# Layer 1 of a four-layer network: router and low-rank columns moved behind the FFN's in one three-bank product, expert choice one pair later

## The reference, cut to what matters

```
base_out   = h @ base_w.T + base_b          # 1024 columns
res_hidden = h @ A.T                        # R1 = 64 columns (low rank)
logits     = h @ router_w.T                 # E1 = 16 columns (router)
topw, topi = top_k(softmax(logits), 2);  topw = topw / (sum(topw) + 1e-6)
combine    = sum over the two chosen experts of one_hot(topi) * topw
out        = base_out + 0.5 * einsum(combine, res_hidden, B)      # B: 16 x 1024 x 64
```

## Time and profile before

| | us |
|---|---|
| median of three runs (lowest, highest) | 2204.11 (2204.09, 2206.6) |
| the profiled execution, whole | 2207.09 |
| its span, first to last instruction | 2205.3 |
| TensorE busy in the span | 2032.4 (92%) |
| VectorE / ScalarE / GpSimd busy | 1183.8 / 885.6 / 388.3 |
| mean granted TensorE clock | 0.964 |

### The profile page before, as it was taken

The page is one execution under the profiler, slowest core; times in us unless marked ns, Lnnn a source line. Parts: engine busy times, 40 slices in busy tenths (PEclk is TensorE's granted clock), DMA queues, the critical chain, the costliest instruction groups (busy, mean ns, idle before and its releaser), DMA issues. The chain is left out here.

```text
span 2205.3 us, 29894 instructions
## 1 busy us (share of the span) xinstructions
PE 2032.4 (92%) x9742; PEld 1665.3 (76%) x9750; DVE 1183.8 (54%) x1986; ACT 885.6 (40%) x1366; POOL 388.3 (18%) x463
## 2 busy tenths in 40 slices
PE   4899956899999979997999999988999999979998
PEld 4777723788888868886788888867888778858886
DVE  6888888745445443224644445436555444454443
ACT  4577722444433321002433333324666544413441
POOL 4122211111111100012111111111000033342334
PEclk9999989899999989997999999998999999989999
DMA  7666546321112232224311111212111011132114
GB/s 185 187 182 181 167 162 216 101 75 57 57 57 71 63 124 76 77 95 135 99 57 57 57 57 61 63 49 81 29 38 33 15 53 50 46 132 78 50 43 156
DMA packets 96302, 196.97 MB, mean 89 GB/s; under 512 B 16768, under 2 KB 46976, under 8 KB 95488
## 3 DMA queue, kind: packets, MB, share of 16 engines
q1 hardware_dynamic: 94976, 194.40, 28.2%
q10 hardware_dynamic: 1280, 1.97, 0.4%
HBM read 142.27 MB, written 54.07 MB: 89 GB/s over the span
## 5 line engine op out<-in xcount | busy, mean ns | idle before, releaser
L936 PE MATMUL ps<-l_u_hi,l_g_hi 128*128 128x512 f32 x512 | 208.9, 408 | 15.7 <-DVE l_u_lo L1270 10.1
L1100 ACT ACTIVATE l_hs<-ps,l_EY,dem3e 128x512 f32<-128x512 f32 x128 | 99.2, 778 | 302.4 <-PE ps L936 292.4
L936 PE MATMUL ps<-l_u_lo,l_g_hi 128*128 128x512 f32 x512 | 204.7, 400 | 0.0
L936 PE MATMUL ps<-l_u_hi,l_g_lo 128*128 128x512 f32 x512 | 204.2, 399 | 0.0
L119 POOL TENSOR_TENSOR l_hs<-l_EY,ones 128x4 f32<-128x4 f32 x128 | 35.0, 273 | 860.1 <-ACT l_hs L1100 860.1
L989 PE MATMUL ps<-l_w_hi,l_h_hi 128*128 128x512 f32 x512 | 167.7, 409 | 0.0
L989 PE MATMUL ps<-l_w_lo,l_h_hi 128*128 128x512 f32 x512 | 163.7, 401 | 0.0
L989 PE MATMUL ps<-l_w_hi,l_h_lo 128*128 128x512 f32 x512 | 163.1, 400 | 0.0
L2228 POOL TENSOR_TENSOR f_a_lo<-f_prod,f_a_hi 128x512 fp32r<-128x512 f32 (+1 forms) x88 | 113.8, 1293 | 269.2 <-ACT f_a_hi L2131 269.2
L2184 DVE SCALAR_TENSOR_TENSOR f_prod<-ps,b,f_gate 128x512 f32<-128x512 f32 (+1 forms) x88 | 66.0, 750 | 170.0 <-ACT f_gate L2124 170.0
L1270 DVE SCALAR_TENSOR_TENSOR l_u_lo<-ps,s_u,l_u_hi 128x512 fp32r<-128x512 f32 x128 | 95.5, 749 | 89.1 <-ACT l_u_hi L1082 88.9
(11 more groups left out here) (326 smaller groups left out, 4892.3 us busy)
## 6 DMA issues: line engine op xcount, KB each, us to landing
xin<-x SPq DMA_DIRECT2D x96, 256.0 KB, 4.0
l_xr<-x SPq DMA_DIRECT2D x32, 512.0 KB, 4.6
x<-l_xr SPq DMA_DIRECT2D x32, 512.0 KB, 2.6
v<-in_ffn_v SPq DMA_DIRECT2D x84, 128.0 KB, 2.7
xin<-in_x SPq DMA_DIRECT2D x16, 512.0 KB, 5.5
xb<-in_x SPq DMA_DIRECT2D x16, 512.0 KB, 3.2
x<-xb SPq DMA_DIRECT2D x16, 512.0 KB, 2.6
q_xr<-x SPq DMA_DIRECT2D x16, 512.0 KB, 3.9
```

The costliest lines, as they stand in the source:

```text
L936: mm = nc.tensor.matmul(ps[:, 3 + h, :], Gs[ws][:, h, at:at + P], Us[ms][:, h, 1 + q:1 + q + HALF], start=(k == 0), stop=(k == 11))
L1100: nc.scalar.activation(hs[:, h, :], ps[:, 3 + h, :], ACT.Identity, bias=EY[:, 1, 0, bass.ds(h * NP + p, 1)], scale=dem3e[:, bass.ds(h * NP ...
```

## The change

1. The weights of layer 1 become one matrix of 1104 columns: FFN 0 to 1023, then the low-rank and the router columns. `ffn` multiplies it in three products of THIRD = 368 columns, into banks 5, 6 and 7. The small product is gone.
2. The expert choice is taken out of the tail into the functions `route` (VectorE) and `route_exp` (ScalarE), with one step less at its start. Pair p−1's choice is made in the tail of pair p, pair 15's in `expert_delta`.
3. The end of the tail: a copy of the 80 small columns out of bank 7, the sum of banks 5 and 6 (736 columns), a wait for that one, the sum of bank 7's other REST = 288 columns.
4. Tiles that the choice needs now live through both phases; some semaphores are counted from another start.

```diff
+THIRD = (L + R1 + E1) // 3
+REST = L - 2 * THIRD
+ROUTE_LINKS = 13
...
-            wsp = sb2("w", [P, KB, L])
-            both_m = sb("m", [P, KB, 2 * SMALL[layer]], F32R)
+            if layer == 1:
+                wsp = sb2("w", [P, KB, 3 * THIRD])
+                msp = [t[:, :, L:3 * THIRD] for t in wsp]
...
                 if first and layer < 3:
                     wait_lo(pe, 0)
+                if layer == 1:
+                    if not first:
+                        pe.wait_ge(xo_ready, r0 + p)
+                    for b in range(KB):
+                        if first:
+                            wait_lo(pe, b + 1)
+                        for ws, ms in PASSES:
+                            for o in range(3):
+                                mm = nc.tensor.matmul(ps[:, 5 + o, 0:THIRD], hsp[ws][:, b, :],
+                                                      wsp[ms][:, b, o * THIRD:(o + 1) * THIRD],
+                                                      start=(k == 0), stop=(k == 3 * KB - 1))
+                            k += 1
+                    mm.then_inc(ffn_done, 1)
+                    return
...
             def tail(p):                      # ScalarE
-                if layer == 1:
-                    act.wait_ge(side[0], side0[0] + p + 1)
-                    nc.scalar.activation(ex[:, :], small[:, R1:R1 + E1], ACT.Exp, bias=nmax[:, :],
-                                         accum_out=esum[:, :]).then_inc(side[1], 1)
+                if layer == 1 and not (isinstance(p, int) and p == 0):
+                    route_exp(nc, act, kept, p - 1, sem)
...
                 if layer == 1:                # VectorE, tail(p)
-                    dve.wait_ge(small_done, r0 + p + 1)
-                    link(0, v.tensor_copy(small[:, :], ps[:, 7, 0:SMALL[1]]))
-                    link(1, v.tensor_tensor(small[:, :], small[:, :],
-                                            ps[:, 7, SMALL[1]:2 * SMALL[1]], ALU.add))
...
+                    if not (isinstance(p, int) and p == 0):
+                        route(nc, dve, kept, p - 1, sem)
+                    dve.wait_ge(ffn_done, r0 + p + 1)
+                    v.tensor_copy(kept["small"][:, :], ps[:, 7, REST:THIRD]).then_inc(small_read, 1)
+                    dve.wait_ge(xr_biased, r0 + p + 1)
+                    planes = in_planes(xr[:, :])
+                    x2 = planes[:, :, 0:THIRD].rearrange("p s (c m) -> p s c m", c=2)
+                    by_rest = planes[:, :, THIRD:HALF]
+                    v.tensor_tensor(x2, ps[:, 5:7, 0:THIRD].rearrange("p c (m s) -> p s c m", s=2), x2,
+                                    ALU.add).then_inc(x_part, 1)
+                    dve.wait_ge(x_part, r0 + p + 1)
+                    dve.wait_ge(small_read, r0 + p + 1)
+                    v.tensor_tensor(by_rest, ps[:, 7, 0:REST].rearrange("p (m s) -> p s m", s=2), by_rest,
+                                    ALU.add).then_inc(xo_ready, 1)
+                    return
...
+def route(nc, dve, kept, p, sem):
...
+    dve.wait_ge(sem("small_read"), p + 1)
+    carry(0)
+    link(0, v.max(top[:, :], small[:, R1:R1 + E1]))
+    v.tensor_copy(kept["res"][:, bass.ds(p, 1), :], small[:, 0:R1].unsqueeze(1))
+    v.tensor_scalar(nmax[:, :], top[:, 0:1], -1.0, None, ALU.mult).then_inc(nmax_ready, 1)
+    dve.wait_ge(ex_ready, p + 1)
+    link(1, v.reciprocal(den[:, 0:1], esum[:, :]))
...
+    link(12, v.tensor_tensor(kept["comb"][:, bass.ds(p, 1), :].rearrange("p a e -> p (a e)"),
+                             prob[:, :], ex[:, :], ALU.add))
...
+def route_exp(nc, act, kept, p, sem):
+
+    act.wait_ge(sem("side0"), p + 1)
+    nc.scalar.activation(kept["ex"][:, :], kept["small"][:, R1:R1 + E1], ACT.Exp, bias=kept["nmax"][:, :],
+                         accum_out=kept["esum"][:, :]).then_inc(sem("side1"), 1)
...
                 split_b(k)                    # expert_delta, ScalarE
+            route_exp(nc, act, kept, NP - 1, sem)
             hi(1, 1, True)
...
                                 ALU.subtract).then_inc(b_lo, 1)      # expert_delta, VectorE
+            route(nc, dve, kept, NP - 1, sem)
             lo(1, 1)
             build(2, 0, False)
```

More of the change, by code:

```diff
@@ L210, in program @@
                     keep_sb("b_raw", [P, AHEAD, L], F32)
+                    keep_sb("small", [P, SMALL[1]], F32)
+                    for name, width in (("iota", E1), ("top", 8), ("nmax", 1), ("ex", E1), ("esum", 1), ("prob", E1),
+                                        ("indexf", 2), ("den", 2), ("pick", 2), ("carrier", 3)):
+                        keep_sb(name, [P, width], F32)
+                    keep_sb("index", [P, 8], U32)
                 if layer == 3:
@@ L566, in conv_phase @@
         if with_ffn:
-            carrier = sb("carrier", [P, 3])
             bias = sb("bias", [P, L])
-            wsp = sb2("w", [P, KB, L])
-            both_m = sb("m", [P, KB, 2 * SMALL[layer]], F32R)
-            msp = [both_m[:, :, i * SMALL[layer]:(i + 1) * SMALL[layer]] for i in range(2)]
-            small = sb("small", [P, SMALL[layer]])
+            if layer == 1:
+                wsp = sb2("w", [P, KB, 3 * THIRD])
+                msp = [t[:, :, L:3 * THIRD] for t in wsp]
+            else:
+                carrier = sb("carrier", [P, 3])
+                wsp = sb2("w", [P, KB, L])
+                both_m = sb("m", [P, KB, 2 * SMALL[2]], F32R)
+                msp = [both_m[:, :, i * SMALL[2]:(i + 1) * SMALL[2]] for i in range(2)]
+                small = sb("small", [P, SMALL[2]])
         if layer == 3:
@@ L629, in conv_phase @@
             for k in range(KB):
-                chunks.append((w_dram[k], [t[:, k, :] for t in wsp], L))
+                chunks.append((w_dram[k], [t[:, k, 0:L] for t in wsp], L))
         if layer == 2:
@@ L695, in conv_phase @@
         if layer < 3:
-            chain, chain_len = sem(lay + "chain"), 13 + layer
+            chain, chain_len = sem(lay + "chain"), 15
         if with_ffn:
@@ L699, in conv_phase @@
                 "bias_loaded", "small_read", "ffn_done", "xr_loaded", "xr_biased", "xo_ready", "x_stored"))
+        if layer == 1:
+            x_part = chain
         if layer == 2:
@@ L969, in ffn @@
                     else:
-                        for ws, m in ((0, 2 * SMALL[layer]), (1, SMALL[layer])):
+                        for ws, m in ((0, 2 * SMALL[2]), (1, SMALL[2])):
                             mm = nc.tensor.matmul(ps[:, 7, 0:m], hsp[ws][:, b, :], both_m[:, b, 0:m],
@@ L990, in ffn @@
                                                   wsp[ms][:, b, o * HALF:(o + 1) * HALF],
-                                                  start=(k == 0), stop=(layer == 1 and k == 3 * KB - 1))
+                                                  start=(k == 0), stop=False)
                         k += 1
@@ L1406, in tail @@
[L1406 to L1421, removed]
```

46 lines of the change are left out of this document (25 added, 21 removed).

## The result

| | before | after |
|---|---|---|
| median, us (lowest, highest) | 2204.1 (2199.76, 2206.6), 6 runs | 2196.91 (2193.65, 2198.79), 6 runs |
| ratio, 95% interval | | 0.9965 [0.9954, 0.9976] |
| profiled execution: span | 2205.3 | 2197.0 |

A forecast was written before the change was run, and what follows sets the result against it. TensorE, busy throughout layer 1's steady pairs, was taken as the bound. Terms −12.5 − 3.0 + 0.4 + 0.8 gave −14.3 us, a median of 2189.8; forecast 2186 to 2194 (79%), 8-in-10 range 2186 to 2197.

The forecast's parts named there:

- step 3: VectorE's tail in layer 1: ends 0.38 us later, under the 0.58 slack before `weights_g`, so TensorE loses nothing.
- step 1: Layer 1's product in steady pairs 1 to 13: 12.13 us instead of 13.09, gaining 0.96 a pair, 12.5 us together.
- rival of a late VectorE: Tail 1.1 us later, stalling TensorE 0.5 us in each of 14 pairs: 7 us come back, about 2197; chance 11%.
- step 2: Product in pairs 0, 14 and 15, partly at half clock: gains 1.0 us each, 3.0 us together.
- step 7: TensorE's clock: pair 14's fall may vanish (−1.7 us), expert_delta's new wait may bring one (+1.7); taken as 0, ±1.7.
- step 4: Expert choice beside the FFN product: stays hidden with over 6 us to spare; a repeated ScalarE table load costs nothing.
- step 5: Last pair of layer 1: no next pair covers pair 15's tail, so the phase ends 0.4 us later.
- step 6: expert_delta: pair 15's choice, 3.9 us on VectorE against 3.15 slack, makes TensorE wait once, +0.8 us.

The follow-up runs named there:

- Experiment 10: Kernel after, with `al` made before the product wait, pair 15's choice behind `G` of pair 3, and the product waiting for `h_hi` first: 2184.17 us, ratio 0.9903.
- experiment 1: Kernel after, with VectorE making `al` of the pair after next before it waits for the product: 2191.79 us, ratio 0.9945.
- experiment 2: Kernel after, with VectorE's 16 pairs of layer 1 written out instead of looped: 2192.03 us, ratio 0.9951.
- experiment 3: Kernel after, without VectorE's waits between the tail's instructions; SyncE and TensorE wait for both sums instead: 2193.92 us, ratio 0.9958.
- Experiment 4: Kernel before, with only the tail's 1024-column sum replaced by a copy of 80, sums of 736 and 288, and one wait: 2206.14 us, ratio 1.0011.
- experiment 8: Kernel before with only the later expert choice, and `w` put back on multiples of 64 bytes by two unused tiles: 2204.7 us, ratio 0.9995.
- experiment 6: Kernel before with only the expert choice made one pair later, product and tail unchanged: 2196.23 us, ratio 0.996.
- experiment 7: Kernel before with two unused 32-byte tiles around `w`, so it starts 32 bytes past a multiple of 64: 2196.12 us, ratio 0.9959.
- experiment 12: Experiment 10's kernel with `w` of layer 2 moved to 32 bytes past a multiple of 64 and layer 1's onto a multiple: 2179.93 us, ratio 0.9879.
- experiment 5: Experiment 4's kernel with a second wait, for the copy, ahead of the last sum: 2207.72 us, ratio 1.001.

## Why the prediction was right or wrong

The direction held, and so did the product's part of the mechanism. The forecast −14.3 became −7.2; step 3 failed, and step 1 was mis-sized by a tenth. The range reached to 2197 only for the rival of a late VectorE. That rival's mechanism is the one that occurred, but its sizes are not, so that 2196.9 fell inside the range is partly luck.

**Step 1, the product.** 0.168 us per product as forecast. The rule weighed there from the Trainium skill ("TensorE: Matmul & The Clock Gate", "Back-to-back issue gap") would have given 0.156 for 368 columns; the trace stays with 0.168. The start was under-sized: the first group of three takes 0.62 instead of 0.505 after the wait for `h_lo`, so 0.115 and not 0.04 is lost. Together the gain is 0.84 to 0.88 a pair and not 0.96, below the step's lower bound of 0.90, some 1.3 us over 13 pairs. Experiment 10 confirms the wait as the cause: with the earlier half waited for, the product takes 12.11 and its first group 0.50. Before, the same wait stood ahead of the small product (0.25), whose loads set the pace, and a slow start hardly shows: its first two products take 0.24 us, the next two 0.23.

**Step 3, VectorE's tail, is the step that failed.** Its durations were right to 0.01 us and its end to 0.03. Its claim "0.38 later, less than 0.58: nothing on TensorE" missed that VectorE goes round its loop between the tail and `al`. Before, the sum of 1.22 us hid that: `al` starts as the sum ends. With a wait and a last sum of 0.46 it shows, 0.38 us in each turn. So `al` comes 0.79 later (T + 1.34 to T + 2.13), 0.21 over the slack. TensorE loses that at `weights_g` (0.27 by its starts) and 0.11 to 0.13 more, since after a wait its first products are slower: 0.40 in most turns (24.58 against 24.18), 4.6 us over the 12 turns. Experiments 1 to 3 each take away one condition (place, loop, wait), and all reach 24.18. Experiment 4 shows that the slack was over-sized too: 0.50 of delay already costs 0.08 a pair. The trace of before had the row to suspect it: slack was the distance of two starts, with a loop turn inside whose length no row gave. The rival "VectorE late in each pair" had the place and, at 2197, the time, but by sizes that did not occur.

**Steps 2 and 7, pairs 0, 14, 15 and the clock.** Against experiment 8, which has the small product, `w` in its old place and no fall in pair 14 either, the product is worth 14.66 − 13.78 = 0.88 in pair 0 (the clock is 0.72 from 424 to 430 in both) and 25.01 − 24.18 = 0.83 in pair 14, where 1.0 each was forecast. In pair 15 it can't be read apart from the clock. The fall in pair 14 is absent from the profile of after, as step 7 held possible, but not by the change: it is absent too in experiments 4 and 8, which have the small product, and present in 6 and 7. And the 4.3 us ahead of the first product belong to the profile of before. Where the clock falls changes from run to run; that it came to nothing in the medians was assumed and is not shown.

**Step 4, the choice.** Worth nothing, as experiment 8 shows (0.9995). The table load is repeated as suspected, and hidden, but not ahead of `Exp` and not because the tables alternate: it stands at the first activation (L1094) of each of the loop's 12 turns. The first, at 424.68, comes before any `Exp`; pairs 13 to 15, which run the same `Exp` outside the loop, have none. Rows of ScalarE after: the first turn's load, one pair, and the sum over the kernel (count | total us, mean ns):

```profile
424.68 1.28 ACT L1094 ACT_TABLE_LOAD   x1
...
525.76 0.31 ACT L1677 ACTIVATE ex<-small,nmax 128x16 f32<-128x16 f32 x1 [1.79 <-DVE nmax L1654]
525.98 0.19 ACT L1677 ACTIVATION_READ_ACCUMULATOR ex<-small,nmax 128x1 f32 x1
526.18 1.28 ACT L1094 ACT_TABLE_LOAD   x1
```
```profile
L1094 ACT ACT_TABLE_LOAD x12 | 15.4, 1283 | 0.2
```

15.4 us of loads that cost no time, while TensorE is in the product.

**Steps 5 and 6.** +0.43 (0.4 forecast) and +0.74 (0.8 forecast). The chain on VectorE, 823.42 to 827.21, is 3.8 us, where the working has 3.9. That step 6 came out to the tenth is luck in part: its 3.15 us of slack were read in a run with 0.83 as the granted clock from 827 to 833, and the wait itself became 1.80 us and not 0.8.

**The account.** −14.3, + 4.6 for step 3, + 1.3 for step 1 is −8.4; measured −7.2 in the medians. The 1.2 left is less than the six runs of the kernel after spread (5.1 us); it is not traced further.

**What the prediction could not hold.** The kernel before had a product slowed by the place of its operand. Measured against the same kernel with two unused tiles ahead of it (24.72 a pair), putting the router's columns behind the FFN's is worth 0.54 us a pair at its best (24.18) and 0.14 as it stands (24.58), and in layer 2 it leaves 0.25 a pair lying: as a whole, 2196.9 against 2196.1, nothing. The change also moved `w` to the good place, but 368 columns draw no gain from it (experiment 12).

**Open.** Why the turn costs 0.17 us in the kernel before with the new tail (experiments 4 and 5) and in experiment 1, and 0.39 in the kernel after, with the same last three instructions; the number of waits is excluded. Which property of 368 columns (their row of 4416 bytes, the three banks, the width) makes the place indifferent was not tried.

## What to carry to other kernels

Slack read as a distance between two starts must be checked for what is not an instruction in it: a loop turn hides under a long last instruction and shows up when that is split into short ones behind waits; put the part that another engine waits for ahead of the tail, not behind it. Compare layouts before crediting a change: an experiment that only moves tiles (two pads of 32 bytes) tells what of a gain is address. A change that lets a narrow product vanish into a wide one gains the spacing of the loads, and loses the cover that the narrow one gave to a slow start.

## What the runs showed of the hardware

- The 512-column fp32r products of `w` start 234 or 227 ns apart by where `w`, their moving operand, starts: 234 with it on a multiple of 64 bytes, 227 with it 32 bytes past one (133376 against 133408, 134112). All else equal this is 8 us of 2204 (experiments 6 to 8). `B` in expert_delta starts 32 bytes past one before and after (99680, 100448) and has 227 in both. It isn't shown for every operand: the 512-column products of `u`, whose windows start at several columns, are 0.232 us apart on average (12 from 510.47 to 513.25 in the earlier trace rows).
- VectorE's loop turn delays the next instruction by 0.17 (experiments 1, 4 and 5) to 0.39 us (the kernel after, where 0.30 of it is shown as `<-issue`) when it can't be hidden, and by nothing when it can (experiment 3, and the kernel before).
- TensorE's first products after a wait of a few tenths are slower by 0.11 to 0.13 us together, without an idle mark (0.62 instead of 0.505 for the first group of the product, 0.40 instead of 0.28 to 0.30 for that of `weights_g`).
- With the first `Exp` inside ScalarE's loop, a table load of 1.28 us stands at the head of each turn (12 loads, 15.4 us); with the first `Exp` ahead of the loop there is one load, at 420.41. Nothing else stands still for it: `ACTIVATE` follows 0.02 us behind the load (526.18 + 1.28 to 527.48).
